# A three-layer field-interaction kernel: the first layer's left factor read from SBUF and not from a PSUM copy

## What is computed

```python
x0 = inputs; xk = inputs
for idx, (W, b) in enumerate(params):          # W: 39 x fields of xk x 128
    z = jnp.einsum('bhd,bkd,hks->bsd', x0, xk, W) + b[None, :, None]
    z = jax.nn.relu(z)
    if idx != n_layers - 1:
        half = z.shape[1] // 2
        xk = z[:, :half, :]; direct.append(z[:, half:, :])
    else:
        direct.append(z)
logit = jnp.sum(jnp.concatenate(direct, axis=1), axis=-1)
```

## Time and profile before

| quantity | value |
|---|---|
| median of 3 runs | 559.44 us (559.39 to 560.16) |
| the profiled execution's own time | 560.07 us |
| its span in the trace | 558.3 us |
| TensorE matmul busy | 550.0 us, 99% |
| VectorE busy | 528.2 us, 95% |
| ScalarE busy | 381.6 us, 68% |
| GpSimd busy | 518.9 us, 93% |

### The profile page before, as it was taken

One profiled execution on the slowest core, in us unless ns is written; L12 is line 12 of the kernel. 1 busy time (PEld: TensorE's weight loads), 2 busy tenths in 40 slices (PEclk: granted clock), 3 DMA queues, 4 the chain that ended last, 5 costly groups with the idle time before them and its releaser, 6 DMA issues.

```text
span 558.3 us, 6212 instructions
## 1 busy us (share of the span) xinstructions
PE 550.0 (99%) x2012; PEld 378.3 (68%) x2012; DVE 528.2 (95%) x490; ACT 381.6 (68%) x429; POOL 518.9 (93%) x236
## 2 busy tenths in 40 slices
PE   7999999999999999999999999999999999999997
PEld 3346667777777767777777777767677777777765
DVE  4679999999999999999999999999999999999976
ACT  0447685877768687685777777677776867767654
POOL 0349999999999999999999999999999999999995
PEclk8999999999999999999999999999999999999999
DMA  8997382754838276491836738175492836736000
GB/s 329 416 411 320 124 336 74 287 235 172 355 89 328 110 279 258 150 373 63 340 130 214 313 148 340 58 281 238 156 371 73 301 154 234 303 127 225 26 2 9
DMA packets 21633, 122.18 MB, mean 219 GB/s; under 512 B 2528, under 2 KB 3552, under 8 KB 11360
## 3 DMA queue, kind: packets, MB, share of 16 engines
q1 hardware_dynamic: 21312, 121.51, 57.1%
q10 hardware_dynamic: 288, 0.26, 0.2%
HBM read 121.24 MB, written 0.52 MB: 218 GB/s over the span
## 4 chain that ended last, share of the span: by engine, by line
PE 91%; POOL 3%; issue 2%; DVE 1%; ACT 1%; DMA 1%; ACTq 0%
PE z L632 91%; POOL lo L536 3%; DMA raw<-w 1%; DVE exact L445 1%; ACT maps L696 0%; POOL w_lo L552 0%; ACT L696 0%; DVE raw L445 0%; ACT hi L677 0%; ACT final L717 0%; DVE sums L474 0%; DVE w_exact L497 0%; ACTq L295 0%
## 5 line engine op out<-in xcount | busy, mean ns | idle before, releaser
L536 POOL TENSOR_TENSOR lo<-raw,hi 128x1024 fp32r<-128x1024 f32 x206 | 487.7, 2398 | 9.4 <-ACT hi L677 7.7
L677 ACT ACTIVATE hi<-raw 128x1024 fp32r<-128x1024 f32 (+1 forms) x221 | 225.6, 1030 | 121.6 <-DVE raw L445 112.2
L445 DVE TENSOR_TENSOR raw<-spread,maps 128x1024 f32<-128x1024 f32 x192 | 228.3, 1209 | 3.0 <-POOL lo L536 1.5
L632 PE MATMUL z<-hi,w_hi 128*128 128x512 f32 (+1 forms) x563 | 227.7, 409 | 0.0
L632 PE MATMUL z<-hi,w_lo 128*128 128x512 f32 x517 | 203.9, 394 | 0.0
L632 PE MATMUL z<-lo,w_hi 128*128 128x512 f32 x548 | 192.0, 440 | 0.2 <-POOL lo L536 0.2
L632 PE MATMUL z<-exact,w_exact 128*128 128x512 f32 (+1 forms) x378 | 178.0, 598 | 3.2 <-DVE exact L445 2.4
L632 PEld LDWEIGHTS z<-lo,w_hi 128*128 128x128 f32 x548 | 102.5, 188 | 50.6 <-issue 28.7
L632 PEld LDWEIGHTS z<-hi,w_hi 128*128 128x128 f32 (+1 forms) x563 | 105.7, 188 | 32.4 <-issue 7.2
L632 PEld LDWEIGHTS z<-exact,w_exact 128*128 128x128 f32 (+1 forms) x378 | 71.4, 190 | 65.9 <-issue 53.4
L632 PEld LDWEIGHTS z<-hi,w_lo 128*128 128x128 f32 x517 | 97.0, 188 | 23.8 <-issue 0.7
(11 more groups left out here) (21 smaller groups left out, 74.1 us busy)
## 6 DMA issues: line engine op xcount, KB each, us to landing
spread<-x_spread SPq DMA_DIRECT2D x80, 1024.0 KB, 8.2
fields<-x_fields SPq DMA_DIRECT2D x31, 768.0 KB, 6.8
fields<-x_fields SPq DMA_DIRECT2D x15, 512.0 KB, 5.5
w_exact<-w SPq DMA_DIRECT2D x10, 256.0 KB, 14.5
spread<-x_fields SPq DMA_DIRECT2D x1, 768.0 KB, 10.1
raw<-w SPq DMA_DIRECT2D x1, 640.0 KB, 6.7
spread<-x_fields SPq DMA_DIRECT2D x1, 512.0 KB, 10.8
out<-sums SPq DMA_DIRECT2D x8, 64.0 KB, 7.6
```

Source lines behind the costliest of these rows:

```text
L445: nc.vector.tensor_tensor(products, by_field, by[0:rows, :].unsqueeze(1).to_broadcast([rows, tiles, COLS]), ALU.mult).then_inc(ready, 1)
L536: nc.gpsimd.tensor_tensor(low_part(layer, c, k), raw[low_rows(layer, k), PLACE[S][layer, c, k] % RAW_RING, 0:tiles_in(layer, k), :], hi[lo ...
L632: mm = nc.tensor.matmul(z_of(layer, c)[:, :], w[0:rows, :], part[0:rows, :], start=(step == FIRST_STEP[layer, c] and p == 0), stop=(step = ...
L677: nc.scalar.activation(hi[0:rows, count % HI_RING, 0:tiles, :], products, ACT.Copy).then_inc(hi_ready, 1)
```

## The change

The bank `copies`, the semaphore `copies_ready` and ScalarE's 15 copy instructions are removed. The products of layer 0 take the left fields from `fields[:, 0, :]` in SBUF in every chunk. Both inputs of these products are then in SBUF. Nothing else is changed; the arithmetic and its operands' values are the same.

```diff
@@ block.vector, multiply
-                        by = early[:, 0, :] if ahead else copies if c else field_copies
+                        by = early[:, 0, :] if ahead else field_copies
@@ block.vector, the loop over chunks
                 if c < LAST:
-                    dve.wait_ge(copies_ready, c + 1)
                     multiply(0, c + 1, range(0 if c else EARLY, COUPLES[0]))
@@ block.scalar
-            def copy_fields(c):
-                act.wait_ge(fields_loaded[0], (c + 1) * 16)
-                nc.scalar.activation(copies[:, :], field_copies, ACT.Copy).then_inc(copies_ready, 1)
@@ block.scalar, the loop over chunks
                 if c == 0:
                     split_hi(1, 0, range(COUPLES[1]))
-                    copy_fields(1)
...
                 else:
-                    split_hi(1, c, range(0, COPY_AT))
-                    if c < LAST:
-                        copy_fields(c + 1)
-                    split_hi(1, c, range(COPY_AT, COUPLES[1]))
+                    split_hi(1, c, range(COUPLES[1]))
```

More of the change, by code:

```diff
@@ L79 @@
 SUM_DIRECT_AT = 6
-COPY_AT = 7
 FINISH_AT = 2
@@ L255, in cin_kernel @@
         maps2 = pb("maps2", [128, COLS])
-        copies = pb("copies", [128, COLS])
         d_raw = pb("d_raw", [128, 2, COLS])
@@ L269, in cin_kernel @@
         spread_loaded = [sem(f"spread_loaded{s}") for s in range(SPREAD_RING)]
-        copies_ready = sem("copies_ready")
         exact_ready = sem("exact_ready")
```

## The result

The changed kernel takes 633.92 us (median of 4 runs, 633.64 to 634.50), the kernel before 559.41 us beside it. The ratio is 1.133, with a 95% interval of 1.1316 to 1.1345: slower by 74.5 us. The prediction said 629 us, 605 to 658.

The account below looks back on a forecast made before the run. TensorE, VectorE and GpSimd were taken as full at once. VectorE's 33.06 + 5.2 us a chunk exceeds the period by 4.9 us: 560.07 + 68.3 (14 chunks) + 1.1 (chunk 1) = 629.5, stated as 629 us, range 605 to 658.

Parts of the forecast that it names:

- Three engines full at once, VectorE's slack 0.32 us a chunk: Mid-kernel, TensorE, VectorE and GpSimd are all full; VectorE idles 0.32 us and GpSimd 0.13 us a chunk.
- The copy's removal: 0: On ScalarE, dropping 15 copies of 0.60 us, 9 us in all, was counted as saving 0.
- A product waits for the running subtraction, GpSimd gets its turn between two products and is then held for 1 us: Layer-0 products with two SBUF inputs wait for GpSimd's current instruction; GpSimd goes between products, losing 1.0 us; chance 0.76.
- the bounds: How long a long product holds GpSimd: between nothing and the product's reading time, 1.0 us; the latter was taken.
- 5.2 us of waits a chunk: VectorE's waits in a chunk's stretch of four layer-0 products, raising its need from 33.06 to 38.3 us.
- The middle between the two ends: The waits of a stretch taken midway between 3.7 us (no subtraction ready beyond the running one) and 6.8 us.
- The stock of ready subtractions falls: On GpSimd, a period longer by 5 us or more leaves it idle partly, so fewer subtractions stand ready.
- VectorE, not GpSimd, decides: VectorE's 38.3 us a chunk exceeds GpSimd's 37.0 us and sets the period; TensorE waits some 5 us a chunk.
- The rival of products that keep their place behind each other: Successive VectorE products let GpSimd in only at the end; GpSimd's 37.0 us a chunk decides, about 611 us; chance 0.10.
- small-price rival: A stretch waits only for one instruction's remainder and GpSimd loses nothing: 573 to 590 us; chance 0.08.
- no collision: Three long VectorE rows have another cause, so the kernel stays at 560.07 us, runs at 559.5; chance 0.04.
- The signs to look for: Changed profile: product rows up to 3.5 us, small one 3 us, some GpSimd rows 3.4 us, `maps` products 1.21 us.

Follow-up runs that it names:

- e7: Kernel before, with only the small last product of layer 0 (76x512) reading the left fields from SBUF, the others the PSUM copy: 585.47 us, ratio 1.0433.
- e8: Kernel before, with only the first product of a stretch reading the left fields from SBUF, the others the PSUM copy: 598.24 us, ratio 1.0689.
- e2: Kernel before, with the PSUM copy filled only once, in chunk 1, and products still reading PSUM: 559.45 us, ratio 1.000.
- the trials: Separate programs without TensorE: rows of GpSimd subtractions, with VectorE products having two SBUF inputs issued beside them; one product makes four subtractions take 10.2 us, not 9.2.
- e4: Changed kernel with GpSimd's subtractions cut to 16 of 512 columns: 562.27 us, against 561.78 us for the kernel before with the same cut.
- e1: Kernel before, with products reading SBUF while ScalarE still makes its copy, which nobody reads: 633.69 us, ratio 1.131.
- e9: Changed kernel, with ScalarE waiting for the free slot of lo, so each GpSimd subtraction waits for one semaphore instead of two: 633.36 us.
- e5: Changed kernel with layer-0 kinds SDES in the middle chunks too (first product writes SBUF, second PSUM): 626.01 us, against 565.24 us in its control.

## Why the prediction was right, step by step

- **Three engines full at once, VectorE's slack 0.32 us a chunk.** Right. It is the term that closes the sums of the changed kernel, e7 and e8 within 1.5 us.
- **The copy's removal: 0.** Right, measured alone: 559.45 us (e2).
- **A product waits for the running subtraction, GpSimd gets its turn between two products and is then held for 1 us.** Right as the common case. It was read from three small weight instructions; the trials show the wait 45 times and the hold 48 times, and for the hold the full reading time was the right end of the bounds (2.34 to 3.32 us). As a rule for every boundary it is wrong on both sides: products are passed over behind a long row, and with short subtractions GpSimd is passed over between products (e4).
- **5.2 us of waits a chunk.** Measured 77.9 / 14 = 5.6 us, with chunk 1's 1 us in it. The period came to 38.68 us, forecast 38.3. But the parts were mis-sized in opposite ways. The first product waits 2.8 us in the mean, not 1.2 to 2.2, since in five of the fourteen stretches it is passed over at two boundaries. The second waits 1.3 us, not up to 2.3, since behind such a long wait GpSimd has run dry. The small one's 1.2 us and the third's 0 are as worked out. The middle between the two ends was a choice that happened to absorb both, and that is luck: the five stretches with a passed-over product wait 7.0 us each (5.7 + 1.2), those with turns 4.7. An estimate from these rows: with turns throughout, the time would have been 5 x 2.3 = 11.5 us less, some 622 us.
- **The stock of ready subtractions falls.** Right: GpSimd is idle 386.8 - 340.2 = 46.6 us in ten chunks, 4.7 us each, and waits 50.5 us for roundings in the whole run, against 7.7 us before.
- **VectorE, not GpSimd, decides.** Right: VectorE has no idle time in ten chunks. TensorE idles 3.0 us a chunk, not 5: its busy time grew from 33.38 to 35.66 us a chunk, at a mean granted clock of 0.95 against 1.00.
- **The rival of products that keep their place behind each other** is out for these long subtractions (three in a row alternate in the trials), though it is what the five odd stretches look like, and what six of GpSimd's eleven long rows in e4 show. The small-price rival and no collision are out.
- **The signs to look for.** Rows up to 3.5 us for the later products, held subtractions of 3.4 us, `maps` products at 1.21 us: all there. Rows of 7 us for the first product were not foreseen.

The Trainium skill, page "SBUF — State Buffer", section "Who interferes with whom", has the collision of a VectorE instruction with two SBUF inputs and a GpSimd instruction that reads SBUF. The traces agree: rows of 3.4 us for a product and for the subtraction behind it. The section's rule "Issue order, not op shape, decides who blocks." doesn't say who follows at the end of an instruction when both wait; here the five passed-over products made a net 11.5 of the 77.9 us. Nor does it fit the five stretches in which GpSimd's row starts 1.0 us ahead of the first product and is yet the one that is held.

## What to carry to other kernels

Before a VectorE operand is moved from PSUM to SBUF, look at what GpSimd does beside it: a seemingly useless copy to PSUM can be what keeps a two-input instruction out of GpSimd's way. VectorE's wait is set by the length of GpSimd's instructions (0.5 us in all with short ones, 74.5 with long ones; the small product waits up to 3.6 us in e7), and it is hidden inside the row, so compare mean durations of one form rather than idle times. Where VectorE and GpSimd are both full, even one such product a chunk cost 4 to 7% here.

## What the runs showed of the hardware that was not expected

- A product can be passed over at the end of a subtraction, and then waits until GpSimd's unbroken row is over: rows of 7 us in the kernel, 11.9 to 13.2 us in the trials, against 3.4 us for one turn. The same happens the other way: a subtraction of 0.25 us waits through three products, 3.48 us (e4).
- A subtraction whose row starts 1.0 us before three products ends 2.2 us behind the third (6.71 us in all, 574.61 against 572.39 us), about the 2.34 us that it takes alone: it seems to have done nothing until they were through, and the products ran at 1.21 us. Five stretches in four kernels show it (one each in the changed kernel, e1 and e9, two in e5); none of the 48 single trials does.
- TensorE's granted clock fell to the lower of its two levels behind a wait: 0.50, 1.2 GHz, from 306 to 310 us in the changed kernel, behind 2.6 us without work; over ten chunks it is 0.95. No cost shows here, since VectorE has no idle time in these ten chunks.

```profile
306.00:310.00 4.00, 3.79 (x9) 2.49 (x9) 4.00 (x4) 2.47 (x5) 2.71 (x2) 0.50 0.07 14
```
